# Level tables of a gated attention layer: from tables expanded by an engine to tables written run by run by transfers

## The chip, the cores and the metric

The kernel runs on one core of a Trainium2 chip. The metric is the device time of one execution in microseconds, the median of several runs. The engines of the core are TensorE (PE; PEld is its weight load), VectorE (DVE), ScalarE (ACT), GpSimd (POOL) and SyncE (SP), which here only issues transfers.

## What is computed

```python
# x: 8 batches x 1024 tokens x 128; H = 8 heads, LV = 12 levels
x = x + attn(layernorm(x)); x = x + experts(layernorm(x))
# attn, for each batch and head:
g = -softplus(x @ Wg.T + bg); G = cumsum(g, axis=1)
lam = softplus(x @ Wdl.T + Lparam)            # [b, t, h, 12]
decay = exp(G[t] - G[s]) where s <= t else 0
lamw[t, s] = lam[t, lvl(t - s)]               # lvl(0)=0, lvl(d)=floor(log2 d)+1
A = (q @ k.T / sqrt(128)) * decay * lamw
out = layernorm(concat_h(A @ v) @ Wo.T + x) * ln_g + ln_b
# experts: softmax gate, top 2 of 8 experts, weighted sum of y = x @ We[e].T + be[e]
```

## The kernel before

There are NH = 64 heads (8 batches of 8 heads), about 23 us each, and everything is fp32 in two fp32r parts, high and low. A head is a pass over NG = 12 groups (a block of 128 keys by up to 512 queries). Every group has four places, so a head has 48 places (0 to 47) and a batch 384; tables written out by hand or by a planner (`PE_MORE`, `DVE_MORE`, `ACT_MORE`, `POOL_MORE`, `Q_AT`, `V_AT`, `V_HIGH`, `V_LOW`) say at which place of the batch each engine does each extra piece. Every engine runs its list strictly in order.

For a group PE makes the scores (place 0 of the group, three matmuls into `s_ps`), DVE multiplies them with the weights `w_all` (`weigh`, `a_all`), ACT rounds the product to fp32r (`a_hi`), POOL subtracts to get the rest (`low_a`, `a_lo`, line 596), and LAG = 4 groups later PE multiplies with the values (`values`, line 1320, into `o_ps`; it waits for `a_lo`).

The weights `w_all` are exp(level logarithm + decay) and are made one head ahead, in five units (`unit(n + 1, u)` in head n, at places 2, 14, 22, 30 and 42). A unit is a chain of small f16 matmuls into `l_ps` (line 1251). Their moving operand is a table: `ra` for levels 0 to 7 and `rb` for levels 8 to 10; their stationary operand is a constant 0/1 mask. In the table each row stands for (part, level, offset q), and the row is zero except at the tokens whose offset within a run of TA = 8 (or TB = 16) tokens is q. A head has 16 matmuls of 64 columns and 16 of 56 that read `ra`, and 8 of 112, 8 of 96, 8 of 64, 2 of 320 and 2 of 192 that read `rb`: 5,120 columns. ACT then takes the exponential (`exps`, line 714), and a unit waits for the one before it to be taken.

The tables are made so: the level logarithms are stored to HBM (`ea_scratch`, `eb_scratch`) in an order in which the tokens of one offset are contiguous; SP loads them compactly (`load_e_part`, four transfers a head, lines 411 and 414) into `ea` and `eb`; POOL multiplies them, broadcast over q, with a 0/1 constant (`expand_a` at place 10, line 581, and `expand_b` at place 21, line 587). In `ra` and `rb` q is the innermost index, so a matmul reads runs of 8 or 16 contiguous f16 elements.

SP's queue in each head n, in order: at head 0 of a batch `store_out` of an earlier batch and `load_residual` (into `yx`, used by POOL's `shifted_x`, piece `xb`); at head 5 `load_x`; then `load_m(n + 3)`; at head 4 `store_el`; then `load_e(n + 4)`; in odd heads `load_n`. POOL also does most of the work of the two normalisations (`dev1`, `t_dev`, `apply1`, `t_apply`, `scale`, `xb`, `add`, `dev2`, `apply2`, `total`).

## Time and profile before

| | |
|---|---|
| median of 3 runs | 1608.88 us (1608.41 to 1609.42) |
| the profiled execution, its own time | 1608.22 us |
| its span, first to last instruction | 1606.1 us |
| granted TensorE clock, mean | 0.968 of full speed |
| PE, ACT, POOL, DVE busy | 91%, 71%, 71%, 64% |
| HBM traffic | 26 GB/s over the span |

A busy share is the time in which an engine has at least one instruction in work. The rows further down show single lines, engines and stretches: how long an instruction takes, and how long an engine sat idle before it and what ended the idle time.

### The profile page before, as it was taken

Reading aid. Unit: us, or ns where it says so; the run is one execution under the profiler, and the core shown is the slowest. Engines: PE = TensorE matmul, PEld = TensorE weight load, DVE = VectorE, ACT = ScalarE, POOL = GpSimd, SP = SyncE. Lnnn points to the kernel's source line nnn. Section 1 sums busy time; section 2 is a strip of 40 time slices with the busy share of each in tenths; the row PEclk is TensorE's granted clock in tenths of the full one; section 3 lists DMA queues with packets and bytes.
Section 4 is the critical chain, followed back from the end, with each engine's and each line's share of the span. In section 5 each row is a group of like instructions: output and inputs, shape, how many; then the busy total and the mean of one; then the engine's idle time right before and its main releaser. Section 6 shows DMA issues by size and latency. Waiting matters only on the chain.

```text
span 1606.1 us, 29807 instructions
## 1 busy us (share of the span) xinstructions
PE 1456.4 (91%) x10678; PEld 1210.6 (75%) x10678; DVE 1030.0 (64%) x2466; ACT 1141.3 (71%) x3299; POOL 1143.1 (71%) x1067
## 2 busy tenths in 40 slices
PE   5799997899989999899989999899998999989975
PEld 5588886778867887777877788678786887878853
DVE  5457565676657766586655866467674676647665
ACT  2689886786768767686766967678676886867631
POOL 1486779766896678956798667975679666896570
PEclk8799999999999999999999999999999999999987
DMA  5200100010100101001010010001010000100000
GB/s 176 64 18 16 39 28 15 10 37 20 36 15 7 38 22 36 13 15 42 10 35 13 25 36 20 23 16 35 23 36 12 10 26 19 36 16 28 8 8 13
DMA packets 80332, 44.01 MB, mean 27 GB/s; under 512 B 21832, under 2 KB 78522, under 8 KB 80058
## 3 DMA queue, kind: packets, MB, share of 16 engines
q1 hardware_dynamic: 79484, 41.83, 9.2%
q8 instruction: 85, 1.39, 0.4%
q14 instruction: 61, 0.50, 0.1%
q10 hardware_dynamic: 702, 0.29, 0.1%
HBM read 32.39 MB, written 9.18 MB: 26 GB/s over the span
## 4 chain that ended last, share of the span: by engine, by line
PE 55%; POOL 18%; DVE 12%; ACT 9%; issue 4%; DMA 1%; ACTq 0%; SPq 0%; POOLq 0%; DVEq 0%
PE o_ps L1320 15%; PE l_ps L1251 7%; PE s_ps L1235 6%; POOL a_lo L596 6%; PE s_ps L1237 6%; PE s_ps L1236 6%; PE aux L1235 4%; ACT w_all L714 4%; PE aux L1236 4%; PE aux L1237 4%; DVE a_all L912 2%; ACT a_hi L737 2%; POOL ra L581 2%; POOL e_rs L602 1%; POOL yx L441 1%
## 5 line engine op out<-in xcount | busy, mean ns | idle before, releaser
L596 POOL TENSOR_TENSOR a_lo<-a_all,a_hi 128x512 fp32r<-128x512 f32 (+2 forms) x640 | 709.1, 1125 | 323.9 <-ACT a_hi L737 322.7
L912 DVE TENSOR_TENSOR a_all<-s_ps,w_all 128x512 f32<-128x512 f32 (+3 forms) x768 | 422.6, 554 | 488.4 <-PE s_ps L1237 476.3
L714 ACT ACTIVATE w_all<-l_ps,bias 128x128 f32<-128x128 f32 x2304 | 628.5, 386 | 58.1 <-PE l_ps L1251 57.5
L737 ACT ACTIVATE a_hi<-a_all 128x512 fp32r<-128x512 f32 (+2 forms) x640 | 364.0, 591 | 254.8 <-DVE a_all L912 251.5
L1320 PE MATMUL o_ps<-a_hi,v_all 128*128 128x512 f32 (+2 forms) x1280 | 472.1, 373 | 56.9 <-POOL a_lo L596 56.8
L1320 PEld LDWEIGHTS o_ps<-a_hi,v_all 128*128 128x128 f32 x1280 | 243.9, 191 | 110.5 <-POOL a_lo L596 72.5
L1235 PE MATMUL s_ps<-q_hi,xt_hi 128*128 128x512 f32 (+3 forms) x768 | 290.4, 378 | 2.5 <-DVE a_all L912 2.5
L1236 PE MATMUL s_ps<-q_lo,xt_hi 128*128 128x512 f32 (+3 forms) x768 | 268.3, 349 | 0.0
L1237 PE MATMUL s_ps<-q_hi,xt_lo 128*128 128x512 f32 (+3 forms) x768 | 268.0, 349 | 0.0
L1320 PE MATMUL o_ps<-a_lo,v_all 128*128 128x512 f32 (+2 forms) x640 | 232.4, 363 | 0.0
L1237 PEld LDWEIGHTS s_ps<-q_hi,xt_lo 128*128 128x128 f32 x768 | 147.0, 191 | 17.1
L1235 PEld LDWEIGHTS s_ps<-q_hi,xt_hi 128*128 128x128 f32 x768 | 147.6, 192 | 15.9 <-DVE a_all L912 4.0
L1251 PE MATMUL l_ps<-rb,mask 96*128 96x112 f16 (+4 forms) x1792 | 134.7, 216 | 25.3 <-ACT w_all L714 25.3
L1236 PEld LDWEIGHTS s_ps<-q_lo,xt_hi 128*128 128x128 f32 x768 | 148.2, 193 | 11.3
L1251 PEld LDWEIGHTS l_ps<-rb,mask 96*128 96x128 f16 x1792 | 94.8, 98 | 68.0 <-ACT w_all L714 36.8
L581 POOL TENSOR_TENSOR ra<-ea,cst 128x1024 f16<-128x1024 f16 x64 | 123.3, 1926 | 29.5 <-DMA eb<-eb_scratch 29.5
L1320 PEld LDWEIGHTS o_ps<-a_lo,v_all 128*128 128x128 f32 x640 | 122.5, 191 | 12.0
L587 POOL TENSOR_TENSOR rb<-eb,cst 96x1024 f16<-96x1024 f16 x64 | 123.0, 1923 | 0.0
L899 DVE TENSOR_TENSOR v_all<-aux,v_all 128x512 fp32r<-128x512 f32 x128 | 87.3, 682 | 24.2 <-ACT v_all L729 24.2
L891 DVE TENSOR_TENSOR q_lo<-aux,q_hi 128x512 fp32r<-128x512 f32 x128 | 88.5, 691 | 4.4
L1251 PEld LDWEIGHTS l_ps<-ra,mask 128*128 128x128 f16 x2048 | 75.1, 98 | 18.2 <-issue 2.9
L889 DVE CAST q_hi<-aux 128x512 fp32r<-128x512 f32 x128 | 87.7, 685 | 0.4 <-PE aux L1237 0.3
(175 smaller groups left out, 2216.1 us busy)
## 6 DMA issues: line engine op xcount, KB each, us to landing
mt<-m_scratch SPq DMA_DIRECT2D x62, 128.0 KB, 2.0
nt<-n_scratch SPq DMA_DIRECT2D x62, 128.0 KB, 2.6
tx<-in_L_attn_x SPq DMA_DIRECT2D x9, 512.0 KB, 4.1
out<-yn SPq DMA_DIRECT2D x16, 256.0 KB, 2.3
yx<-in_L_attn_x SPq DMA_DIRECT2D x7, 512.0 KB, 4.2
ea<-ea_scratch SPq DMA_DIRECT2D x126, 16.0 KB, 1.9
eb<-eb_scratch SPq DMA_DIRECT2D x126, 6.0 KB, 1.8
ea_scratch<-tx SPq DMA_DIRECT2D x15, 128.0 KB
```

The costliest lines, as they stand in the source:

```text
L581: pool.tensor_tensor(ra[k][:, :, :, :].rearrange("p i n q -> p (i n) q"), ea[k][:, :, None].broadcast_to([P, P, TA]), c("dma")[:, None, :] ...
L587: pool.tensor_tensor(rb[k][:, :, :, :].rearrange("p i n q -> p (i n) q"), eb[k][:, :, None].broadcast_to([KB, NC * NTB, TB]), c("dmb", KB) ...
L596: pool.tensor_tensor(a_lo[r][:, 0:t1 - t0], a[r][:, 0:t1 - t0], a_hi[r][:, 0:t1 - t0].bitcast(F32), ALU.subtract).then_inc(a_lo_done, 1)
L714: last = act.activation(w[k][:, W_AT[j] + dd, :].rearrange("p (f c) -> p f c", f=2), l_ps[:, :, slot * HF:(slot + 1) * HF], ACT.Exp, bias= ...
L737: act.activation(a_hi[r][:, 0:t1 - t0], a[r][:, 0:t1 - t0], ACT.Copy).then_inc(a_hi_done, 1)
L891: dve.tensor_tensor(q_lo[n % 2][:, cols], bank(piece), q_hi[n % 2][:, cols].bitcast(F32), ALU.subtract).then_inc(freed(piece), 1)
L912: dve.tensor_tensor(a[(n * NG + g) % NA][:, 0:t1 - t0], s_ps[:, g % 2, 0:t1 - t0], w[n % 2][:, at:at + (t1 - t0) // P, :].rearrange("p i n ...
L1235: pe.matmul(o, a_hi, hi, start=True, stop=False)
L1236: pe.matmul(o, a_hi, lo, start=False, stop=False)
L1237: return pe.matmul(o, a_lo, hi, start=False, stop=True)
L1251: r = pe.matmul(o, lhsT, rhs, start=not started[f], stop=True, skip_group_check=True)
L1320: last = pe.matmul(o, lhs[:, vr, j, :], rhs[r][:, 0:t1 - t0], start=False, stop=True, skip_group_check=True)
```

## The change

The compact tiles `ea` and `eb`, the two expansions on POOL and their constants are gone. `ra` and `rb` are set to zero once at the start by four memsets on POOL. After that, every head's transfers write only the run of each offset q: 8 transfers of 16 rows of 256 bytes for `ra` (`load_ra`), and 16 transfers of 6 rows of 128 bytes for `rb` (`load_rb`), 24 in place of 4. In the tables q is now the outermost index of a row, so that a run is contiguous; the matmuls read them through a rearranged view, with q innermost, where neighbouring columns are 256 bytes (`ra`) or 128 bytes (`rb`) apart. The order of the rows (level, part, offset) and of the scratch tensors changes to fit. A head's transfers (`load_levels(n + 3)`) now wait for `l_mm`, the last unit of the head that used the buffer before, which runs at place 42; before, `load_e(n + 4)` waited for `expand_b` at place 21. At the start the transfers are shared out between SP and ACT. The planner's tables differ: two `t_apply` and one `apply2` pieces (two tiles each) of each batch go from POOL to ACT, and many pieces of all engines move by a few places.

```diff
-    l_a, q_a = (row // TA % LOW)[:, None, None], (row % TA)[:, None, None]
+    l_a, q_a = (row // 2 % LOW)[:, None, None], (row // (2 * LOW))[:, None, None]
...
     rb = np.arange(KB)
-    l_b, q_b = (rb // TB % HIGH + LOW)[:, None, None], (rb % TB)[:, None, None]
+    l_b, q_b = (rb // 2 % HIGH + LOW)[:, None, None], (rb // (2 * HIGH))[:, None, None]
...
-    put("dma", (row % TA)[:, None] == np.arange(TA)[None, :])
-    put("dmb", (rb % TB)[:, None] == np.arange(TB)[None, :])
...
-    ea_dram = nc.dram_tensor("ea_scratch", [B, 2, H * LOW, T], F16, kind="Internal").ap()
-    eb_dram = nc.dram_tensor("eb_scratch", [B, 2, H * HIGH, T], F16, kind="Internal").ap()
+    ea_dram = nc.dram_tensor("ea_scratch", [B, H * LOW, 2, T], F16, kind="Internal").ap()
+    eb_dram = nc.dram_tensor("eb_scratch", [B, H * HIGH, 2, T], F16, kind="Internal").ap()
     with ExitStack() as outer:
...
-Q_AT = {6: 0, 20: 1}
-V_AT = {11: 0, 26: 1, 36: 2, 46: 3}
-V_HIGH = {9: 0, 28: 1, 37: 2, 45: 3}
-V_LOW = {18: 0, 32: 1, 41: 2, 49: 3}
-EXPAND_A, EXPAND_B = 10, 21
+Q_AT = {5: 0, 20: 1}
+V_AT = {11: 0, 26: 1, 40: 2, 46: 3}
+V_HIGH = {9: 0, 27: 1, 40: 2, 45: 3}
+V_LOW = {19: 0, 32: 1, 41: 2, 50: 3}
...
-ACT_MORE = {13: [('y', 0)], 24: [('y', 1)], 92: [('t_high', 0)], 120: [('t_high', 1)], 124: [('x_high', 0)],
-            128: [('x_high', 1)], 136: [('abs', 0)], 140: [('num', 0)], 156: [('exp', 0)], 162: [('ln', 0)],
-            186: [('lnl', 0)], 204: [('l_high', 0)], 220: [('l_high', 1)]}
...
+ACT_MORE = {8: [('y', 0)], 28: [('y', 1)], 52: [('t_apply', 2)], 70: [('t_apply', 1)], 96: [('t_high', 0)],
+            104: [('apply2', 3)], 121: [('x_high', 0)], 124: [('t_high', 1)], 132: [('x_high', 1)],
+            141: [('abs', 0)], 145: [('num', 0)], 161: [('exp', 0)], 165: [('ln', 0)], 186: [('lnl', 0)],
+            196: [('l_high', 0)], 209: [('l_high', 1)]}
...
-POOL_MORE = {32: [('dev1', 0)], 37: [('xb', 0)], 41: [('t_dev', 0)], 44: [('xb', 1)],
-             48: [('apply1', 0), ('apply1', 1)], 49: [('scale', 0)], 52: [('apply1', 2), ('apply1', 3)],
-             56: [('add', 0)], 60: [('scale', 1)], 61: [('add', 1)], 69: [('t_apply', 0)], 73: [('t_apply', 1)],
-             77: [('t_apply', 2)], 81: [('t_apply', 3)], 93: [('dev2', 0)], 96: [('apply2', 0)], 97: [('apply2', 1)],
...
+POOL_MORE = {29: [('xb', 0)], 32: [('dev1', 0)], 33: [('apply1', 1)], 36: [('xb', 1)], 40: [('t_dev', 0)],
+             48: [('apply1', 0)], 49: [('apply1', 2), ('scale', 0)], 56: [('add', 0)], 57: [('apply1', 3)],
+             60: [('scale', 1)], 64: [('t_apply', 0)], 73: [('add', 1)], 81: [('t_apply', 3)], 93: [('dev2', 0)],
+             100: [('apply2', 2)], 101: [('apply2', 0)], 105: [('apply2', 1)], 284: [('total', 0)],
+             369: [('total', 1)]}
...
-        ea = [sb(f"ea{k}", [P, P], F16) for k in range(2)]
-        eb = [sb(f"eb{k}", [KB, NC * NTB], F16) for k in range(2)]
-        ra = [sb(f"ra{k}", [P, NC, NTA, TA], F16) for k in range(2)]
-        rb = [sb(f"rb{k}", [KB, NC, NTB, TB], F16) for k in range(2)]
+        ra = [sb(f"ra{k}", [P, TA, NC, NTA], F16) for k in range(2)]
+        rb = [sb(f"rb{k}", [KB, TB, NC, NTB], F16) for k in range(2)]
...
-        E_IN, EL = 4 * 16, 4 * 16
+        RA_IN, RB_IN, EL = TA * 16, TB * 16, 4 * 16
...
         def store_el_part(eng, b, part):
             src = (elt_hi, elt_lo)[part]
-            eng.dma_start(ea_dram[b, part], src[0:NA_ROWS, :]).then_inc(t["stored"], 16)
-            eng.dma_start(eb_dram[b, part], src[NA_ROWS:NE_ROWS, :]).then_inc(t["stored"], 16)
-
-        def load_e_part(eng, n, part):
+            eng.dma_start(ea_dram[b, :, part], src[0:NA_ROWS, :]).then_inc(t["stored"], 16)
+            eng.dma_start(eb_dram[b, :, part], src[NA_ROWS:NE_ROWS, :]).then_inc(t["stored"], 16)
+
+        def load_ra(eng, n, qs):
             b, h = divmod(n, H)
-            k = n % 2
-            eng.dma_start(ea[k][part * LOW * TA:(part + 1) * LOW * TA, :],
-                          ea_dram[b, part, h * LOW:(h + 1) * LOW, :]
-                          .rearrange("l (q n) -> (l q) n", q=TA)).then_inc(e_in[k], 16)
-            eng.dma_start(eb[k][part * HIGH * TB:(part + 1) * HIGH * TB, :],
-                          eb_dram[b, part, h * HIGH:(h + 1) * HIGH, :]
-                          .rearrange("l (q n) -> (l q) n", q=TB)).then_inc(e_in[k], 16)
+            for q in qs:
+                eng.dma_start(ra[n % 2][q * 2 * LOW:(q + 1) * 2 * LOW, q].rearrange("r i t -> r (i t)"),
+                              ea_dram[b, h * LOW:(h + 1) * LOW, :, q * T // TA:(q + 1) * T // TA]
+                              .rearrange("l r t -> (l r) t")).then_inc(ra_in[n % 2], 16)
+
+        def load_rb(eng, n, qs):
+            b, h = divmod(n, H)
+            for q in qs:
+                eng.dma_start(rb[n % 2][q * 2 * HIGH:(q + 1) * 2 * HIGH, q].rearrange("r i t -> r (i t)"),
+                              eb_dram[b, h * HIGH:(h + 1) * HIGH, :, q * T // TB:(q + 1) * T // TB]
+                              .rearrange("l r t -> (l r) t")).then_inc(rb_in[n % 2], 16)
         EL_ROWS = ((0, NA_ROWS, TA), (NA_ROWS, NE_ROWS, TB))
...
                     for part in range(2):
                     for part in range(2):
                         store_el_part(sp, b, part)
-                def load_e(n):
+                def load_levels(n):
                     if n >= 2:
-                        sp.wait_ge(rb_ready, n - 1)
+                        sp.wait_ge(l_mm, NU * (n - 1))
                     sp.wait_ge(t["stored"], EL * (n // H + 1))
-                    for part in range(2):
-                        load_e_part(sp, n, part)
+                    load_ra(sp, n, range(TA))
+                    load_rb(sp, n, range(TB))
                 def load_last_x():
...
                 sp.wait_ge(t["el_lo"], 2)
                 store_el_part(sp, 0, 1)
                 sp.wait_ge(t["stored"], EL)
-                for n in range(2):
-                    load_e_part(sp, n, 1)
+                sp.wait_ge(zeroed, 4)
+                load_ra(sp, 0, range(TA))
+                load_rb(sp, 0, range(HALF_B, TB))
+                load_ra(sp, 1, range(TA))
                 sp.wait_ge(s_hi, 2)
                 sp.wait_ge(s_lo, 2)
                 first_n()
                 store_weights(1)
                 sp.wait_ge(s_mst, 16)
+                load_rb(sp, 1, range(TB))
                 load_m(2)
-                for n in range(2, 4):
-                    load_e(n)
                 sp.wait_ge(s_nst, 64)
                 load_n(1)
                 load_x(1)
+                load_levels(2)
                 for n in range(NH):
                     b, h = divmod(n, H)
                     if h == 0:
...
                         load_m(n + 3)
                     if h == 4 and b + 1 < B:
                         store_el(b + 1)
-                    if n + 4 < NH:
-                        load_e(n + 4)
+                    if n + 3 < NH:
+                        load_levels(n + 3)
                     if n % 2 and n + 3 < NH:
                         load_n((n + 1) // 2 + 1)
...
             @block.gpsimd
             def _(pool):
-                def expand_a(n):
-                    k = n % 2
-                    pool.wait_ge(e_in[k], E_IN * (n // 2 + 1))
-                    if n >= 2:
-                        pool.wait_ge(l_mm, NU * (n - 1))
-                    pool.tensor_tensor(ra[k][:, :, :, :].rearrange("p i n q -> p (i n) q"),
-                                       ea[k][:, :, None].broadcast_to([P, P, TA]),
-                                       c("dma")[:, None, :].broadcast_to([P, P, TA]), ALU.mult).then_inc(ra_ready, 1)
-
-                def expand_b(n):
-                    k = n % 2
-                    pool.tensor_tensor(rb[k][:, :, :, :].rearrange("p i n q -> p (i n) q"),
-                                       eb[k][:, :, None].broadcast_to([KB, NC * NTB, TB]),
-                                       c("dmb", KB)[:, None, :].broadcast_to([KB, NC * NTB, TB]),
-                                       ALU.mult).then_inc(rb_ready, 1)
-
                 def low_a(n, g):
                     j, t0, t1 = GROUPS[g]
...
                 pool.memset(minus, -1.0).then_inc(s_ones, 1)
                 pool.memset(mhalf[:, :], -0.5).then_inc(ready, 1)
+                for k in range(2):
+                    pool.memset(ra[k][:, :, :, :], 0.0).then_inc(zeroed, 1)
+                    pool.memset(rb[k][:, :, :, :], 0.0).then_inc(zeroed, 1)
                 pool.wait_ge(ready, 2)
                 token_deviation(0)
                 for i0 in range(HC, NC, 2):
                     token_apply(pool, 0, i0)
-                for n in range(2):
-                    expand_a(n)
-                    expand_b(n)
                 for n in range(NH):
                     b, h = divmod(n, H)
                     for place in range(4 * NG):
                         if place % 4 == 1 and place // 4 in SPLIT:
                             low_a(n, place // 4)
-                        if place == EXPAND_A and n + 2 < NH:
-                            expand_a(n + 2)
-                        if place == EXPAND_B and n + 2 < NH:
-                            expand_b(n + 2)
                         more(b, 4 * NG * h + place)
                 for f in range(2):
                     shifted_x(B - 1, f)
...
                 act.wait_ge(t["el_hi"], 4)
                 store_el_part(act, 0, 0)
                 act.wait_ge(t["stored"], EL)
-                for n in range(2):
-                    load_e_part(act, n, 0)
+                act.wait_ge(zeroed, 4)
+                load_rb(act, 0, range(HALF_B))
                 act.activation(mhalf_exp[:, :], mhalf[:, :], ACT.Exp).then_inc(s_exp, 1)
                 act.wait_ge(s_n, 1)
                 act.activation(mn[:, :, 2, :], per_head(pn[:, :]), ACT.Copy).then_inc(s_hi, 1)
...
                 def unit(n, u):
                     k = n % 2
                     if u == 0:
-                        pe.wait_ge(ra_ready, n + 1)
+                        pe.wait_ge(ra_in[k], RA_IN * (n // 2 + 1))
                     if u == 1:
-                        pe.wait_ge(rb_ready, n + 1)
+                        pe.wait_ge(rb_in[k], RB_IN * (n // 2 + 1))
                     if n or u:
                         pe.wait_ge(w_done, n * NU + u)
                     started = [False, False]
...
                             for tb in range(NTA):
                                 f, at = divmod(tb * TA, HF)
                                 last = mm(f, l_bank[f][:, :, at:at + TA], m(f"ma{d}")[:, tb * P:(tb + 1) * P],
-                                          ra[k][:, i0:i0 + cnt, tb, :])
+                                          ra[k][:, :, i0:i0 + cnt, tb].rearrange("p q i -> p i q"))
                         if d in (1, 2, 4):
                             for tb in range(NTB):
                                 f, at = divmod(tb * TB, HF)
                                 last = mm(f, l_bank[f][:, :, at:at + TB], m(f"mb{d}", KB)[:, tb * P:(tb + 1) * P],
-                                          rb[k][:, i0:i0 + cnt, tb, :])
+                                          rb[k][:, :, i0:i0 + cnt, tb].rearrange("p q i -> p i q"))
                         if d in (3, 5):
                             for f in range(2):
-                                last = mm(f, l_bank[f], m("m9" if d == 3 else "m10", KB),
-                                          rb[k][:, i0:i0 + cnt, f * NTB // 2:(f + 1) * NTB // 2, :].rearrange(
-                                              "p i n q -> p i (n q)"))
+                                last = mm(f, l_bank[f].rearrange("p i (t q) -> p i t q", q=TB),
+                                          m("m9" if d == 3 else "m10", KB),
+                                          rb[k][:, :, i0:i0 + cnt, f * NTB // 2:(f + 1) * NTB // 2].rearrange(
+                                              "p q i t -> p i t q"))
                         slot += cnt
                     last.then_inc(l_mm, 1)
```

## Rows read from the trace of the kernel before

**Rows 1.** The page: span, and busy time of the engines (share of the span).

```profile
span 1606.1 us, 29807 instructions
...
PE 1456.4 (91%) x10678; PEld 1210.6 (75%) x10678; DVE 1030.0 (64%) x2466; ACT 1141.3 (71%) x3299; POOL 1143.1 (71%) x1067
```

**Rows 2.** Busy time in stretches: the steady one, then two neighbouring heads.

```profile
core 0: us, PE busy (x) PEld busy (x) DVE busy (x) ACT busy (x) POOL busy (x), PEclk, DMA share, GB/s
64.00:1563.00 1499.00, 1395.22 (x10412) 1164.48 (x10411) 974.37 (x2292) 1110.51 (x3230) 1124.97 (x1041) 0.98 0.08 23
...
801.25:821.04 19.79, 19.19 (x150) 15.96 (x149) 15.02 (x49) 15.71 (x49) 15.75 (x13) 1.00 0.22 63
821.04:848.00 26.96, 20.78 (x152) 17.02 (x151) 11.81 (x26) 16.93 (x51) 26.82 (x32) 0.94 0.03 7
```

**Rows 3.** Waits of PE, 64 to 1563 us (us in total, times, longest).

```profile
PE o_ps L1320 <- POOL a_lo L596: 56.8, 62, 2.1
PE l_ps L1251 <- ACT w_all L714: 20.8, 25, 2.3
PE aux L1364 <- POOL tx L441: 6.7, 6, 1.2
```

**Rows 4.** Groups of instructions by line: the expansions.

```profile
L581 POOL TENSOR_TENSOR ra<-ea,cst 128x1024 f16<-128x1024 f16 x64 | 123.3, 1926 | 29.5 <-DMA eb<-eb_scratch 29.5
L587 POOL TENSOR_TENSOR rb<-eb,cst 96x1024 f16<-96x1024 f16 x64 | 123.0, 1923 | 0.0
```

**Rows 5.** Timeline of PE, the second unit of a steady head (start, length).

```profile
806.40 0.58 PE L1251 MATMUL l_ps<-ra,mask 128*128 128x56 f16 x16
806.81 0.56 PE L1251 MATMUL l_ps<-rb,mask 96*128 96x112 f16 x8
807.18 0.36 PE L1235 MATMUL s_ps<-q_hi,xt_hi 128*128 128x256 f32 x1
```

**Rows 6.** Timeline of PE, the same unit at the start, clock at its lower level.

```profile
50.89 0.97 PE L1251 MATMUL l_ps<-ra,mask 128*128 128x56 f16 x16
51.68 0.93 PE L1251 MATMUL l_ps<-rb,mask 96*128 96x112 f16 x8
52.38 0.56 PE L1235 MATMUL aux<-nt,xt_hi 128*128 128x256 f32 x1
```

**Rows 7.** Groups by line: DVE reads with a stride (L997) and without (L912).

```profile
L997 DVE TENSOR_TENSOR tx<-aux,tx 64x512 f16<-64x512 f32 x16 | 10.8, 674 | 0.0
L912 DVE TENSOR_TENSOR a_all<-s_ps,w_all 128x512 f32<-128x512 f32 x384 | 264.0, 688 | 330.2 <-PE s_ps L1237 319.9 <-ACT w_all L714 9.1
L912 DVE TENSOR_TENSOR a_all<-s_ps,w_all 128x128 f32<-128x128 f32 x128 | 36.6, 286 | 42.8 <-PE s_ps L1237 42.8
```

**Rows 8.** One line's transfers: issue time on SP's queue (min/median/max ns).

```profile
L411 SPq DMA_DIRECT2D ea<-ea_scratch x126: 450/460/1541, 39.9 to 1461.2; - x126
L414 SPq DMA_DIRECT2D eb<-eb_scratch x126: 579/584/1549, 40.4 to 1461.7; - x126
```

**Rows 9.** Timeline of SP's queue: the start, and head 0 of a batch.

```profile
39.92 0.48 SPq L411 DMA_DIRECT2D ea<-ea_scratch  x1
...
46.38 1.33 SPq L482 DMA_DIRECT2D nt<-v_all  x2
...
811.47 0.40 SPq L498 DMA_DIRECT2D yx<-in_L_attn_x  x1
```

**Rows 10.** The page's transfers (KB each, us from issue to landing).

```profile
yx<-in_L_attn_x SPq DMA_DIRECT2D x7, 512.0 KB, 4.2
```

**Rows 11.** Groups by line: one normalising step on POOL and on ACT.

```profile
L441 POOL TENSOR_SCALAR yx<-yn,e_rs,e_sh 128x128 f32<-128x128 f32 x56 | 24.5, 449 | 0.7
...
L786 ACT ACTIVATE yx<-yn,e_sh,e_rs 128x128 f32<-128x128 f32 x8 | 3.3, 482 | 7.3 <-POOL e_sh L617 7.3
```

**Rows 12.** Timeline of POOL and of ACT in the first 60 us.

```profile
9.25 1.67 POOL L602 TENSOR_TENSOR t_rs<-t_ve,mhalf 128x8 f32<-128x8 f32 x1 [8.15 <-DVE t_ve L435]
...
53.41 0.60 ACT L729 ACTIVATE v_all<-aux 128x512 fp32r<-128x512 f32 x1 [4.50 <-DMA n_scratch<-v_all]
```

More of the change, by code:

```diff
@@ L69 @@
 for _name, _n in (("ma0", NTA * P), ("ma1", NTA * P), ("mb1", NTB * P), ("mb2", NTB * P), ("mb4", NTB * P),
-                  ("m9", P), ("m10", P), ("ident", P), ("tri", P), ("suf", P), ("dma", TA), ("dmb", TB),
-                  ("first", E), ("neg", P)):
+                  ("m9", P), ("m10", P), ("ident", P), ("tri", P), ("suf", P), ("first", E), ("neg", P)):
     CONST[_name] = (_at, _at + _n)
@@ L165 @@
 NE_ROWS = NLV * H
+HALF_B = TB // 2
 NGATE = 18
@@ new lines @@
+V_AT = {11: 0, 26: 1, 40: 2, 46: 3}
+Q_OUT = {12: 0, 22: 1}
+V_HIGH = {9: 0, 27: 1, 40: 2, 45: 3}
+V_LOW = {19: 0, 32: 1, 41: 2, 50: 3}
+PE_MORE = {9: [('Y', 0)], 21: [('Y', 1)], 90: [('T', 0)], 110: [('Z', 0)], 122: [('X', 0), ('T', 1)],
[4 rows of a table added]
+DVE_MORE = {5: [('t_stat', 0), ('t_stat', 1)], 13: [('t_stat', 3)], 16: [('t_stat', 2)],
+            17: [('o', 1), ('stat1', 0)], 29: [('stat1', 2), ('stat1', 3)], 32: [('stat1', 1)], 33: [('mean1', 0)],
+            44: [('t_mean', 0)], 77: [('stat2', 1), ('stat2', 0)], 88: [('stat2', 3)], 93: [('stat2', 2)],
+            100: [('mean2', 0)], 101: [('t_low', 0)], 113: [('z', 0)], 120: [('t_low', 1)], 129: [('x_low', 0)],
+            141: [('z', 1), ('x_low', 1)], 145: [('gate', 0)], 152: [('gate', 1)], 169: [('gate', 2), ('gate', 3)],
+            173: [('softplus', 0), ('softplus', 1)], 177: [('guard', 0)], 181: [('sums', 0)], 189: [('decay', 0)],
+            196: [('log', 0)], 197: [('log', 1)], 205: [('l_low', 0)], 220: [('l_low', 1)], 221: [('up', 0)],
[3 rows of a table added]
@@ L341, in main_stage @@
         s_cat, s_rows, s_fwg, s_wes, s_wetc = (sem(n) for n in ("s_cat", "s_rows", "s_fwg", "s_wes", "s_wetc"))
-        e_in, m_in = ([sem(f"{n}{k}") for k in range(2)] for n in ("e_in", "m_in"))
-        ra_ready, rb_ready, l_mm, w_done = sem("ra_ready"), sem("rb_ready"), sem("l_mm"), sem("w_done")
+        ra_in, rb_in, m_in = ([sem(f"{n}{k}") for k in range(2)] for n in ("ra_in", "rb_in", "m_in"))
+        l_mm, w_done, zeroed = sem("l_mm"), sem("w_done"), sem("zeroed")
         s_mm, a_done, a_hi_done, a_lo_done = sem("s_mm"), sem("a_done"), sem("a_hi_done"), sem("a_lo_done")
```

10 lines of the change are left out of this document (removed), and 15 rows, old and new, of tables (DVE_MORE, PE_MORE).

## The prediction

> **What bounds the kernel now.** I read the page first, for who is busy, then the busy times by stretch, then PE's waits. PE is the busiest engine, 1456.4 of 1606.1 us [rows 1]. In the steady stretch, which is nearly the whole run, it works for 1395.2 of 1499 us, so 103.8 us are idle [rows 2]. The reader is to see there how uneven this is: one head takes 19.8 us with PE busy for 19.2 and POOL for 15.8, and the next takes 27.0 us with PE busy for 20.8 and POOL for 26.8. That second head is set by POOL, the others by PE. The waits agree: of PE's idle time 56.8 us end with POOL's `a_lo`, 6.7 with POOL's normalised `tx` and 20.8 with ACT's exponentials [rows 3]. So two prices matter: what each PE column costs in 63 heads, and what POOL carries in about one head of eight.
>
> **POOL's share, removed.** The two expansions take 1.93 and 1.92 us a head, 246 us in all [rows 4]. Six tiles a batch leave POOL as well: 6 x 0.449 = 2.7 us a batch, 19 us over seven batches [rows 11]. The POOL-bound stretch of each batch loses up to two heads' expansions (7.7 us) and those 2.7 us, more than the 6.2 us that PE idles there [rows 2]. The gain can't exceed the waits on POOL, 56.8 + 6.7 = 63.5 us. A part stays, since `a_lo` also waits for ACT and DVE before it: I take 80% of the 63.5, -51 us (bounds: 0, if ACT's `a_hi` is late instead, to -64).
>
> **ACT's share, added.** The same six tiles cost 0.482 us each there [rows 11], 2.9 us a batch, 20 us in all. ACT is idle for 389 us of the steady stretch [rows 2], which covers them; without cover they delay an exponential that PE waits for. I take +5 (0 to +20) where PE isn't slower, and nothing where it is.
>
> **PE's columns, slower.** The matmuls of a head's units read 5,120 columns. Nothing is added in columns, instructions or weight loads, but the moving operand, until now runs of 8 or 16 adjacent f16 elements, becomes one element every 256 or 128 bytes. No matmul in this trace reads so; the price has to be bounded. The second unit shows today's: its 16 x 56 and 8 x 112 columns, 1,792, take from 806.40 to 807.18, 0.78 us or 0.435 ns a column; they are set by columns, since half the instructions take the same time when each has twice the columns [rows 5]. Lower bound: a stride is free, as on DVE, where a read with a stride of 32 bytes takes 674 ns and a contiguous one of 512 elements 688 [rows 7]. That DVE, however, takes an element only every (688 - 286) / 384 = 1.05 ns, and no engine here takes separate elements at PE's 0.435. Upper bound: PE gets them no faster than DVE, 1.05 ns a column: 5,120 x 0.61 = 3.1 us a head, +197 over 63 heads. Between the two lies the rate at which PE itself runs at its lower clock, where the same unit takes 50.89 to 52.38, 1.49 us or 0.83 ns a column [rows 6]. I take this one: it is the nearest row of the same instructions, and close to the pace at which DVE gets single elements. It costs 0.71 us on 1,792 columns, 2.03 us on 5,120, and +128 us over 63 heads (the first head's units run mostly at the lower clock already). PE is the bound in most heads, so nothing hides it; what it hides is the idle time of PE, since others now have 2 us more a head: with it half of the 20.8 us of waits on ACT goes, -10.
>
> The Trainium skill, "Advanced Engine Details and Errata", section "SBUF Cachelines", says that a line holds 16 bytes and that two hits on it are needed for full speed, and speaks of a penalty where each access goes to another line. Before, the runs fill whole lines; after, every column is on another one. The page gives no size. By it the sum is on the slow side; without it the sum is that of the first rival. DVE's strided read, which is from PSUM, doesn't show the penalty at DVE's own pace, so the trace neither confirms nor refutes the rule for PE.
>
> **SP's queue.** Issuing one table transfer takes 0.46 to 0.58 us [rows 8]. A head had four, 2.1 us; now 8 x 0.46 + 16 x 0.58 = 13.0 us, of a head of 20 to 27 us, so SP keeps up. They start after the unit at place 42 and end some 13 us on, about place 24 of the next head; the table is wanted a whole head later. What lies behind them is late: `load_n` (has another head's time), `store_out`, and `load_residual` in head 0 of a batch. It was issued at 811.47, 10.2 us after that head's first unit [rows 2, 9]; it now goes out about 12 us after, and lands 4.2 us later [rows 10], at 16. POOL wants it at place 29 (before, 37), which at 0.41 us a place (19.8 / 48) is 11 us after. POOL's `a_lo`s then queue behind `xb`, for up to 5 us, of which the lag of four groups (6.6 us less some 3 us of work) absorbs most: +10 for seven batches (0 to +25).
>
> **The start.** SP issued 4 transfers from 39.92 and then `first_n` at 46.38 [rows 9]. Now 16 `ra` runs and 8 `rb` runs stand ahead: 7.4 + 4.6 = 12.0 us, so `first_n` goes at 51.9, +5.5 us. ACT waited for the stores behind it until 53.41 [rows 12], so this is on the path. ACT's own 8 transfers, some 5 us from 39.9, end before. The memsets stand on POOL where it idles for 8.15 us before 9.25 [rows 12]; even at an expansion's 1.92 us each, four take 7.7. The first unit no longer waits for an expansion, but for seven more issues. I take +5.5 (0 to +8).
>
> The bytes stay the same (32 KB and 12 KB a head) at a DMA share of 0.08 [rows 2]: no cost. The other moved pieces change no work; nothing for them, +-5.
>
> **Sum.** Against the profiled execution's own 1608.2 us: +128 -51 -10 +10 +5.5 = 1690.7; its run lies 0.7 below the median of the runs shown, so I write 1690.
>
> **Rivals.** First, the stride is free for PE. Then 1608.2 -51 +5 +10 +5.5 +0.7 = 1578, faster by 1.9%. For it: PE already reads fp32r at the same pace as f16, so bandwidth in bytes isn't tight, and DVE's stride costs nothing. Against it: no row shows separate elements delivered in 0.435 ns. It turns at a price of about 0.1 ns a column: 5,120 x 63 x 0.1 = 32 us eat the gain; below that it decides for faster.
> Second, SP becomes the bound: if an issue with only 6 rows takes 1 us instead of 0.58, a head needs 8 x 0.46 + 16 + 1.5 = 21 us of queue, more than the light heads of 19.8; with buffers late in half of the heads by 1 to 2 us and a free stride, about 1578 + 50 = 1628; with the stride's price it is partly hidden. Against: the slowest median issue in the trace is 0.58.
> Third, the work leaves POOL but PE's waits turn to ACT's `a_hi` and exponentials (ACT gains work, is 74% busy in the steady stretch), with a free or nearly free stride: no gain, 1608 + 5 + 5.5 - 10, about 1608.
> Fourth, single elements come only at DVE's pace: 1690 + 69 = 1759.
>
> **How the numbers follow.** Price of the stride near half pace (between 0.7 and 0.95 ns a column): 0.52, around 1690, own range 1650 to 1720. Slower still: 0.06. Free stride with the gain: 0.32, around 1578. Waits turned or prices that cancel: 0.07, of which 0.05 within the bound of 0.2% (about what can be told from no change here). SP as the bound: 0.03. So slower 0.62, same 0.05, faster 0.33. Because both signs are likely, the range reaches from just below the free stride's 1578 to the top of the likeliest: 1560 to 1720.
>
> **What would show it.** The first look is the second unit's matmuls: 16 of 56 columns and 8 of 112 that take 1.5 us from first to the next group's scores, not 0.78, and a PE busy time up by some 130 us. If they take 0.8, the forecast is wrong and the first rival right. Right for POOL: busy near 880 us, waits on `a_lo` under 15 us, and the batch's second head no longer 27 us. SP: issues at 0.46 to 0.58, bursts of 13 us, and `xb` idle on the transfer into `yx`. The start: the first scores about 5 us later than now.

## The result, and the profile after

The changed kernel takes 1939.66 us (1930.96 to 1943.26, 4 runs) against 1608.64 us: a ratio of 1.205, interval 1.201 to 1.209. I had said 1690 us and a range of 1560 to 1720. The direction was right, the size was not: the loss is 331 us, where I forecast 81. The profiled execution is the shortest of the four (its own time 1930.96, span 1929.1).

The page of the changed kernel, against [rows 1]; below it the share of PE in the chain that ended last, the chain followed back from the last instruction (before the change PE had 55% of it and POOL 18%):

```profile
span 1929.1 us, 30902 instructions
...
PE 1865.5 (97%) x10678; PEld 1517.9 (79%) x10678; DVE 1021.2 (53%) x2466; ACT 1173.6 (61%) x3341; POOL 890.8 (46%) x901
...
PE 91%; ACT 4%; DVE 2%; DMA 1%; SPq 1%; issue 0%; ACTq 0%; POOL 0%; POOLq 0%; DVEq 0%
PE l_ps L1232 31%; PE o_ps L1302 20%; PE s_ps L1217 7%; PE s_ps L1218 7%; PE s_ps L1216 7%; PE aux L1216 5%; PE aux L1217 5%; PE aux L1218 5%; ACT w_all L695 2%; PE o_ps L1297 1%; ACT L695 0%; ACT L737 0%; PE aux L1377 0%; PE aux L1339 0%; PE aux L1390 0%; PE aux L1389 0%
```

PE has the same 10,678 matmuls and is busy 409 us longer. One line holds 31% of the chain, the level matmuls (L1232; L1251 before). The steady stretch, against [rows 2], and that line alone in it:

```profile
64.00:1880.00 1816.00, 1804.04 (x10429) 1472.46 (x10428) 961.79 (x2271) 1146.88 (x3287) 872.19 (x867) 0.97 0.07 19
...
64.00:1880.00 1816.00, 647.23 (x3917) 407.77 (x3915) 0.97 0.07 19
```

The level matmuls take 647 us here; the same view of the kernel before gives 226.09 us for 3,906 of them, so they are busy 421 us longer. PE as a whole is busy 409 us longer in the stretch and its idle time fell from 103.8 to 12.0 us: the stretch grew by 317 us, and what lies around it by 6, together the 323 us between the two spans. The 421 can't be set beside the 409 as they stand, since a busy time includes the end of each matmul, which overlaps the start of the next. Counted from each matmul's start to the next one's over the whole trace, idle time apart, the matmuls that read `ra` and `rb` take 526.5 us where they took 144.9: +382. All other matmuls take 27 us more, and PE's idle time between matmuls is 86 us less.

PE's timeline in the second unit of a steady head, against [rows 5]:

```profile
927.00 1.79 PE L1232 MATMUL l_ps<-ra,mask 128*128 128x56 f16 x16
928.61 1.73 PE L1232 MATMUL l_ps<-rb,mask 96*128 96x112 f16 x8
930.01 0.56 PE L1216 MATMUL s_ps<-q_hi,xt_hi 128*128 128x256 f32 x1
```

and of the same unit at the start, against [rows 6]:

```profile
54.22 1.83 PE L1232 MATMUL l_ps<-ra,mask 128*128 128x56 f16 x16
55.87 1.73 PE L1232 MATMUL l_ps<-rb,mask 96*128 96x112 f16 x8
57.27 0.56 PE L1216 MATMUL aux<-nt,xt_hi 128*128 128x256 f32 x1
```

The unit takes 3.01 us from first matmul to the next group, 1.68 ns a column in place of 0.435. The start shows how such a price is recognised: the fp32r matmuls around it are at the lower clock, yet the unit takes 3.05 us, the same, where the kernel before took 1.49 us there and 0.78 us at the upper level. The price of these columns doesn't follow PE's granted clock. The two ends of my bound, 0.435 and 1.05 ns, both lay below it.

A second cost follows from the first. Behind the same unit PE's fp32r matmuls are slow for 3.4 us, and the row of that stretch has the granted clock at its lower level (0.51 over these 3.5 us, 1.00 in the 16.7 us behind them):

```profile
930.80 0.63 PE L1302 MATMUL o_ps<-a_hi,v_all 128*128 128x512 f32 x1
931.23 0.63 PE L1302 MATMUL o_ps<-a_lo,v_all 128*128 128x512 f32 x1
...
934.02 0.40 PE L1302 MATMUL o_ps<-a_hi,v_all 128*128 128x512 f32 x1
934.25 0.39 PE L1302 MATMUL o_ps<-a_lo,v_all 128*128 128x512 f32 x1
```

```profile
929.80:933.30 3.50, 3.50 (x12) 2.90 (x11) 0.42 (x1) 2.22 (x8) 0.63 (x1) 0.51 0.00 0
```

The same 512 columns take 0.43 us there and 0.23 us later. Between 80 and 1870 us the clock falls 28 times, and 27 of these falls begin around the last matmul of a head's second unit, none over 1.1 us after its start. What this costs in all is worked out in the experiments.

The groups by line and shape give most of the list (the kernel before had the first two at 41.2 and 37.3 us, and the three of `rb` at 36.0, 33.0 and 26.0; the two shapes left out, 320 and 192 columns, rose from 28.9 and 21.3 to 79.2 and 53.1):

```profile
L1232 PE MATMUL l_ps<-ra,mask 128*128 128x64 f16 x1024 | 129.9, 295 | 0.0
L1232 PE MATMUL l_ps<-ra,mask 128*128 128x56 f16 x1024 | 114.4, 279 | 0.0
L1232 PE MATMUL l_ps<-rb,mask 96*128 96x112 f16 x512 | 110.7, 371 | 0.0
L1232 PE MATMUL l_ps<-rb,mask 96*128 96x96 f16 x512 | 95.0, 340 | 0.7 <-ACT w_all L695 0.7
L1232 PE MATMUL l_ps<-rb,mask 96*128 96x64 f16 x512 | 67.6, 287 | 3.8 <-ACT w_all L695 3.8
```

What PE waited for in the stretch, against [rows 3]; then the timeline of SP's queue with the first value weights at the start and one head's transfers, against [rows 9]; then the transfers' issue times by tile (min/median/max ns), against [rows 8]:

```profile
PE l_ps L1232 <- ACT w_all L695: 8.6, 18, 1.8
PE aux L1339 <- DVE yx L903: 2.9, 1, 2.9
PE o_ps L1302 <- POOL a_lo L581: 0.5, 1, 0.5
```

```profile
49.72 1.32 SPq L481 DMA_DIRECT2D nt<-v_all  x2
...
915.93 3.56 SPq L406 DMA_DIRECT2D ra<-ea_scratch  x8
919.53 5.40 SPq L413 DMA_DIRECT2D rb<-eb_scratch  x16
```

```profile
L406 SPq DMA_DIRECT2D ra<-ea_scratch x512: 302/420/1799, 39.7 to 1802.5; - x171
...
L413 SPq DMA_DIRECT2D rb<-eb_scratch x1016: 257/295/1477, 43.4 to 1808.1; - x170
```

POOL has left PE's waits altogether. SP's 24 transfers take 9.0 us a head, and no wait of PE in the steady stretch ends with them; at the start PE waits for `ra` once, 1.9 us, where it waited 2.2 us for POOL's expansion.

### The profile page after: what moved, and what is told of

It is laid out like the page before. It is cut to its first block, busy times and chain, and to the rows that moved or that the text cites. A ratio compares the mean times of both kernels' runs of the same rounds, so it can differ in the third digit from the quotient of the medians.

```text
span 1929.1 us, 30902 instructions
## 1 busy us (share of the span) xinstructions
PE 1865.5 (97%) x10678; PEld 1517.9 (79%) x10678; DVE 1021.2 (53%) x2466; ACT 1173.6 (61%) x3341; POOL 890.8 (46%) x901
## 4 chain that ended last, share of the span: by engine, by line
PE 91%; ACT 4%; DVE 2%; DMA 1%; SPq 1%; issue 0%; ACTq 0%; POOL 0%; POOLq 0%; DVEq 0%
PE l_ps L1232 31%; PE o_ps L1302 20%; PE s_ps L1217 7%; PE s_ps L1218 7%; PE s_ps L1216 7%; PE aux L1216 5%; PE aux L1217 5%; PE aux L1218 5%; ACT w_all L695 2%; PE o_ps L1297 1%; ACT L695 0%; ACT L737 0%; PE aux L1377 0%; PE aux L1339 0%; PE aux L1390 0%; PE aux L1389 0%
## 5 line engine op out<-in xcount | busy, mean ns | idle before, releaser
L1232 PE MATMUL l_ps<-rb,mask 96*128 96x112 f16 (+4 forms) x1792 | 394.3, 372 | 9.7 <-ACT w_all L695 9.7
L1216 PE MATMUL s_ps<-q_hi,xt_hi 128*128 128x512 f32 (+3 forms) x768 | 314.6, 410 | 0.0
L1232 PEld LDWEIGHTS l_ps<-rb,mask 96*128 96x128 f16 x1792 | 186.5, 111 | 148.5 <-issue 83.4
L1302 PEld LDWEIGHTS o_ps<-a_hi,v_all 128*128 128x128 f32 x1280 | 248.1, 194 | 37.3 <-POOL a_lo L581 4.6
L1217 PE MATMUL s_ps<-q_lo,xt_hi 128*128 128x512 f32 (+3 forms) x768 | 274.9, 358 | 0.0
L1218 PE MATMUL s_ps<-q_hi,xt_lo 128*128 128x512 f32 (+3 forms) x768 | 274.3, 357 | 0.0
L1232 PE MATMUL l_ps<-ra,mask 128*128 128x64 f16 (+1 forms) x2048 | 244.2, 287 | 0.0
L1232 PEld LDWEIGHTS l_ps<-ra,mask 128*128 128x128 f16 x2048 | 220.5, 115 | 16.6 <-issue 0.8
L1216 PEld LDWEIGHTS s_ps<-q_hi,xt_hi 128*128 128x128 f32 x768 | 156.4, 204 | 30.4 <-issue 10.1
L1217 PEld LDWEIGHTS s_ps<-q_lo,xt_hi 128*128 128x128 f32 x768 | 155.1, 202 | 18.6
L1074 DVE SCALAR_TENSOR_TENSOR yn<-aux,gl,yn 128x128 f32<-128x128 f32 x256 | 87.5, 342 | 0.0
```

Source lines behind the costliest of these rows:

```text
L1216: pe.matmul(o, a_hi, hi, start=True, stop=False)
L1217: pe.matmul(o, a_hi, lo, start=False, stop=False)
L1218: return pe.matmul(o, a_lo, hi, start=False, stop=True)
L1232: r = pe.matmul(o, lhsT, rhs, start=not started[f], stop=True, skip_group_check=True)
L1302: last = pe.matmul(o, lhs[:, vr, j, :], rhs[r][:, 0:t1 - t0], start=False, stop=True, skip_group_check=True)
```

## The experiments

Where a kernel reads wrong columns, the bias of the diagonal blocks is also multiplied by 0, so that no exponential overflows; instructions and shapes stay. All times stand beside runs of the kernel before on the same chip.

**Adjacent columns in the changed kernel.** `every` takes n x q columns that are `step` elements apart.

```diff
+                def every(table, step, n, q):
+                    flat = table[:, :, :, :].rearrange("p q i t -> p (q i t)")[:, 0:n * q * step]
+                    return flat.rearrange("p (i q s) -> p i q s", q=q, s=step)[:, :, :, 0]
...
-                                          ra[k][:, :, i0:i0 + cnt, tb].rearrange("p q i -> p i q"))
+                                          every(ra[k], 1, cnt, TA))
...
-                                          rb[k][:, :, i0:i0 + cnt, tb].rearrange("p q i -> p i q"))
+                                          every(rb[k], 1, cnt, TB))
```

> The changed kernel, except that every level matmul reads as many adjacent columns of its table as it read separate ones (the wrong columns of the right table; and the bias of the diagonal blocks is multiplied by 0 so that nothing overflows, so the output isn't the reference's). Transfers, zeroed tables, places and instruction counts stay. Theory A (the loss is PE's reading of single elements, and nothing else): the level matmuls fall from about 638 us of PE busy to about 230, the second unit from 3.0 us to 0.78, and the time is 1560 to 1590 us, the price of my first rival. Theory B (the 24 small transfers a head, their waits, or the new places cost a large part): it stays above 1650 us although PE's matmuls are short again.

Measured: 1548.98 us, ratio 0.962 (0.9603 to 0.9636). The level matmuls take 226.5 us in 64 to 1500 us. With its transfers, zeroed tables, waits and places, the changed kernel would be 60 us faster than the kernel before; its reads cost 391 us. Theory A holds in what it says of the cause, with a time below its range. The level matmuls by shape, as they are when reads cost nothing extra:

```profile
L1236 PE MATMUL l_ps<-ra,mask 128*128 128x64 f16 x1024 | 40.7, 194 | 0.0
L1236 PE MATMUL l_ps<-ra,mask 128*128 128x56 f16 x1024 | 37.3, 188 | 0.0
L1236 PE MATMUL l_ps<-rb,mask 96*128 96x112 f16 x512 | 36.0, 213 | 0.0
```

**The reads alone, in the kernel before.** The compact loads, the expansions on POOL and the places stay.

```diff
-                                          ra[k][:, i0:i0 + cnt, tb, :])
+                                          ra[k][:, :, :, :].rearrange("p i n q -> p (i n q)").rearrange(
+                                              "p (q i t) -> p i q t", q=TA, t=NTA)[:, i0:i0 + cnt, :, tb])
```

(and the same for `rb`)

> The kernel before, with its compact transfers, its expansions on POOL and its places, except that the level matmuls read their tables with the changed kernel's steps (256 or 128 bytes between neighbouring columns; wrong elements, and the diagonal bias multiplied by 0, so the output isn't the reference's). Theory A: 1880 to 1945 us, level matmuls about 640 us busy, the price of the reads on its own being about 5.96 us a head or 375 us, less the idle time of PE that it fills. Theory B: below 1750 us.

Measured: 1966.5 us, ratio 1.222 (1.2202 to 1.2239), somewhat above theory A's range, and 27 us above the changed kernel, whose transfers and places gain something beside the reads. Each shape costs what it does in the changed kernel:

```profile
L1251 PE MATMUL l_ps<-ra,mask 128*128 128x64 f16 x1024 | 130.0, 295 | 0.0
L1251 PE MATMUL l_ps<-ra,mask 128*128 128x56 f16 x1024 | 114.4, 279 | 0.0
L1251 PE MATMUL l_ps<-rb,mask 96*128 96x112 f16 x512 | 110.7, 371 | 0.0
```

So the price belongs to the access pattern, not to who wrote the table. The two runs together rule theory B out. They also show the second cost. PE's time in us over the whole trace, from each matmul's start to the next one's:

| | before | before, reads apart | changed, adjacent | changed |
|---|---|---|---|---|
| level matmuls (`ra`, `rb`) | 144.9 | 527.2 | 146.2 | 526.5 |
| all other matmuls | 1311.1 | 1359.1 | 1286.1 | 1338.6 |
| of these, at the lower clock | 68.9 | 167.0 | 42.2 | 145.5 |
| idle between matmuls | 138.3 | 70.4 | 103.4 | 52.1 |

The two pairs that differ only in the reads agree: the level matmuls take 380 and 382 us more, the others 52 and 48 us more, and the idle time falls by 51 and 68 us. The others have the same columns; what changed is that they spend 103 and 98 us more at the lower clock, where columns take about twice as long, and half of that is their loss. So about 50 of the 391 us are paid by matmuls that don't read these tables. Theory A's range had no such term, and that is why the measured time lies above it.

**Places alone.** The kernel before with the new tables of places.

```diff
-Q_AT = {6: 0, 20: 1}
+Q_AT = {5: 0, 20: 1}
...
-            128: [('x_high', 1)], 136: [('abs', 0)], 140: [('num', 0)], 156: [('exp', 0)], 162: [('ln', 0)],
+            104: [('apply2', 3)], 121: [('x_high', 0)], 124: [('t_high', 1)], 132: [('x_high', 1)],
```

> The kernel before with the changed kernel's tables of places alone (three normalising pieces a batch on ACT, others moved a few places), expansions on POOL kept. My prediction gave the moved pieces nothing (+-5 us) beside the 2.7 us a batch that leave POOL. Theory A: 1590 to 1615 us. Theory B (the places are part of the loss): above 1640 us.

Measured: 1578.93 us, ratio 0.9812 (0.9797 to 0.9827): 30 us faster, below theory A's range. I had priced the moved order at nothing. PE's wait for `a_lo` fell from 56.8 to 42.0 us over the whole run, and the 6.7 us for the normalised `tx` are gone from its longest waits:

```profile
PE o_ps L1320 <- POOL a_lo L596: 42.0, 43, 3.0
PE l_ps L1251 <- ACT w_all L714: 26.8, 22, 2.7
```

**Only the three normalising pieces on ACT**, at places 52, 70 and 104; nothing else of the places.

```diff
-ACT_MORE = {13: [('y', 0)], 24: [('y', 1)], 92: [('t_high', 0)],
+ACT_MORE = {13: [('y', 0)], 24: [('y', 1)], 52: [('t_apply', 2)], 70: [('t_apply', 1)], 92: [('t_high', 0)],
+            104: [('apply2', 3)],
```

> The kernel before with only the three normalising pieces of a batch moved from POOL to ACT (at the changed kernel's places 52, 70 and 104), nothing else. Theory E (the gain of the new places is this relief of POOL in the head that it bounds, at most 2.7 us a batch): 1585 to 1595 us, about 15 to 20 us off. Theory F (the gain comes from when the other pieces are done): 1603 us or more, with the rest of the 30 us in the order.

Measured: 1593.93 us, ratio 0.9906 (0.9891 to 0.992): 15 us. That is theory E's number; the other half of the 30 us is in the order, so neither theory has it alone.

**How far apart may columns be?** Three kernels with `every` at other steps, for `ra` and `rb` (the matmuls of 320 and 192 columns read adjacent ones), and one with adjacent groups of 2 or 4, each on its own 16 bytes:

```diff
+                def groups(table, g, n, q):
+                    flat = table[:, :, :, :].rearrange("p q i t -> p (q i t)")
+                    return flat[:, 0:n * q // g * 8].rearrange("p (i a s) -> p i a s", a=q // g, s=8)[:, :, :, 0:g]
...
-                                          ra[k][:, :, i0:i0 + cnt, tb].rearrange("p q i -> p i q"))
+                                          groups(ra[k], 2, cnt, TA))
...
-                                          rb[k][:, :, i0:i0 + cnt, tb].rearrange("p q i -> p i q"))
+                                          groups(rb[k], 4, cnt, TB))
```

> The kernel of the run adjacent (wrong columns, diagonal bias 0), with neighbouring columns 2 f16 elements (4 bytes) apart for ra and 4 (8 bytes) apart for rb in the units of 64 to 112 columns; the matmuls of 320 and 192 columns read adjacent ones. Theory A1 (the price is set by whether a 16-byte group of the table serves at least two neighbouring columns): no change, 40.7 and 37.3 us busy for ra, 36.0, 32.9 and 25.8 for rb, time about 1549. Theory A2 (PE fetches some bytes per column in proportion to the step, or a step of any kind ends the fast way): rb's three groups at 8 bytes rise clearly, to 1.5 times or more, and ra's too.

> As before with 4 elements (8 bytes) for ra and 8 (16 bytes) for rb. A1: ra unchanged at about 41 and 37 us, rb at the full price of the changed kernel, 110.7, 95.0 and 67.6 us. A2: ra dearer as well, rb perhaps half way.

> 8 elements (16 bytes) for ra, 2 (4 bytes) for rb. A1: ra at the changed kernel's 129.9 and 114.4 us, rb unchanged at 36.0, 32.9 and 25.8. A2: ra below that, since 16 bytes is far less than the 256 of the changed kernel.

> Neighbouring columns in adjacent groups of 2 f16 elements for ra and of 4 for rb, each group 16 bytes from the next (wrong columns, diagonal bias 0). A1: two columns for a fetch, so both tables stay near the fast price (ra 41 and 37 us, rb 36, 33 and 26). If instead each 16-byte group costs a fixed time of some 1.6 ns whatever is taken from it, ra costs 0.8 ns a column, about 75 and 66 us, and rb 0.4, unchanged; this would also explain the 12 us that tiles_inner lies above adjacent, whose groups of 3 to 7 elements come close to that limit.

One execution each: 1588.8, 1728.0, 1679.6 and 1591.1 us, so no time here has an interval. The verdict rests on the second unit in PE's timeline, at the upper level of the clock in all four. `ra` 4 bytes and `rb` 8 bytes apart, then 8 and 16, then 16 and 4, then groups of 2 and of 4:

```profile
713.97 0.58 PE L1236 MATMUL l_ps<-ra,mask 128*128 128x56 f16 x16
714.39 0.98 PE L1236 MATMUL l_ps<-rb,mask 96*128 96x112 f16 x8
715.13 0.37 PE L1216 MATMUL s_ps<-q_hi,xt_hi 128*128 128x256 f32 x1
```

```profile
721.53 1.01 PE L1236 MATMUL l_ps<-ra,mask 128*128 128x56 f16 x16
722.36 1.78 PE L1236 MATMUL l_ps<-rb,mask 96*128 96x112 f16 x8
723.81 0.38 PE L1216 MATMUL aux<-wcat_hi,xt_hi 128*128 128x104 f32 x1
```

```profile
730.41 1.79 PE L1236 MATMUL l_ps<-ra,mask 128*128 128x56 f16 x16
732.02 0.58 PE L1236 MATMUL l_ps<-rb,mask 96*128 96x112 f16 x8
732.42 0.36 PE L1216 MATMUL s_ps<-q_hi,xt_hi 128*128 128x256 f32 x1
```

```profile
713.91 1.01 PE L1236 MATMUL l_ps<-ra,mask 128*128 128x56 f16 x16
714.74 0.58 PE L1236 MATMUL l_ps<-rb,mask 96*128 96x112 f16 x8
715.13 0.36 PE L1216 MATMUL s_ps<-q_hi,xt_hi 128*128 128x256 f32 x1
```

Each of the two parts has 896 columns, so a difference of starts divided by 896 is the time of a column:

| columns side by side in 16 bytes | `ra`, ns a column | `rb`, ns a column |
|---|---|---|
| 4 (step 4 bytes; `rb` also groups of 4) | 0.47 | 0.45, 0.44 |
| 2 (step 8 bytes; `ra` also groups of 2) | 0.93, 0.93 | 0.83 |
| 1 (step 16 bytes) | 1.80 | 1.62 |
| 1 (256 or 128 bytes, the changed kernel) | 1.80 | 1.56 |

Theory A1 fails at its number, two: two columns for each 16 bytes still cost double. A2 fails as well, since 16 bytes cost as much as 256, and a step of 4 bytes nothing. What fits all of it is the alternative in the last expectation: every 16 bytes that a matmul reads cost about 1.6 to 1.8 ns, whatever is taken from them, and a column at least 0.43 ns; from four columns on, the second is the bound. In these runs only one of the two tables is at the full price, and the mean granted clock stays at 0.973 to 0.978, as with adjacent columns; the frequent falls were seen only with both at the full price. Why, the runs don't tell.

**Tiles innermost.** That suggests a version which keeps the direct transfers and reads side by side. The tile index goes last in the scratch order, in the tables and in the PSUM bank; ACT does the stepping.

```diff
-        ra = [sb(f"ra{k}", [P, TA, NC, NTA], F16) for k in range(2)]
+        ra = [sb(f"ra{k}", [P, TA, NTA, NC], F16) for k in range(2)]
...
-            n = T // q // 2
-            return src[r0:r1, :].rearrange("r (q n) -> r q n", q=q)[:, :, f * n:(f + 1) * n]
+            return src[r0:r1, :].rearrange("r (q t i) -> r q t i", q=q, i=NC)[:, :, :, f * HC:(f + 1) * HC]
...
-                                    l_ps[:, :, slot * HF:(slot + 1) * HF], ACT.Exp,
+                                    l_ps[:, :, at * HF:(at + cnt) * HF].rearrange(
+                                        "p f (c i) -> p f c i", i=cnt)[:, :, :, i - i0], ACT.Exp,
...
-                                          ra[k][:, :, i0:i0 + cnt, tb].rearrange("p q i -> p i q"))
+                                          ra[k][:, :, tb, i0:i0 + cnt])
```

> The changed kernel with the tile index innermost, in the scratch order, in the tables and in the PSUM bank of a unit: a run of one offset is still one contiguous transfer, a matmul reads 3 to 8 adjacent f16 elements of one 16-byte group at a time and writes PSUM contiguously, and ACT reads PSUM with a step of 12 to 32 bytes; it computes the reference. Theory A, with the price set by how many neighbouring columns lie side by side: 1560 to 1590 us, level matmuls 230 to 260 us busy. If groups of 3 to 5 elements are too short, the units with 3, 4 and 5 tiles stay slow and the time is 1600 to 1700. Theory B: above 1650. If ACT's stepped read costs, the exponentials' 385 ns goes up by 50 ns or more.

Measured: 1561.77 us, ratio 0.9702 (0.9688 to 0.9717), faster than both kernels. The level matmuls by shape (the 64 columns of `rb` left out), and the exponentials whose read of PSUM is now stepped:

```profile
L1233 PE MATMUL l_ps<-ra,mask 128*128 128x64 f16 x1024 | 40.9, 194 | 0.0
L1233 PE MATMUL l_ps<-ra,mask 128*128 128x56 f16 x1024 | 40.6, 194 | 0.0
L1233 PE MATMUL l_ps<-rb,mask 96*128 96x112 f16 x512 | 39.5, 220 | 0.0
L1233 PE MATMUL l_ps<-rb,mask 96*128 96x96 f16 x512 | 33.2, 208 | 1.6 <-ACT w_all L695 1.6
L1233 PE MATMUL l_ps<-rb,mask 96*128 96x320 f16 x128 | 32.9, 340 | 19.0 <-ACT w_all L695 18.9
L1233 PE MATMUL l_ps<-rb,mask 96*128 96x192 f16 x128 | 25.4, 279 | 0.0
L695 ACT ACTIVATE w_all<-l_ps,bias 128x128 f32<-128x128 f32 x2304 | 631.2, 388 | 54.6 <-PE l_ps L1233 53.8
```

ACT pays nothing (388 ns; 386 in the kernel before). PE pays a little where a group has 7, 5 or 3 columns: 40.6 us for 56 columns against 37.3 with adjacent columns, 39.5 against 36.0 for 112, 32.9 against 28.9 for 320, 25.4 against 21.4 for 192. Groups of 8, 6 and 4 pay nothing (40.9 against 40.7 for 64, 33.2 against 32.9 for 96). From start to start that is 12 us in all, nearly the whole 13 us by which this version lies above the run with adjacent columns. The size is that of one column more in each odd group: two matmuls of the same shape in a row start 29 ns apart for 56 columns as for 64; 175 ns for 320 in fives, and 6/5 of the adjacent 147 is 177; 112 ns for 192 in threes, and 4/3 of 83 is 110. The price of 16 bytes can't explain the 5 and the 7. Each odd group here also starts at an odd column, so the runs don't separate the count from the start.

**The same with the old places.** `V_LOW` and the other tables as in the kernel before.

```diff
-V_LOW = {19: 0, 32: 1, 41: 2, 50: 3}
+V_LOW = {18: 0, 32: 1, 41: 2, 49: 3}
```

> The kernel of the run tiles_inner (reference output) with the tables of places of the kernel before: the transfers' part alone, without its new places and with the price of the reads gone. The places alone took 30 us off the kernel before. Theory C (the two parts free the same resource, POOL, so that their gains overlap): 1562 to 1578 us, less than 30 us worse than tiles_inner. Theory D (they add up): 1588 to 1595 us.

Measured: 1582.7 us, ratio 0.9845 (0.9825 to 0.9864). It lies between the two theories: transfers alone give 26 us, places alone 30, both together 48, so some 8 us are the same. The 26 and the 48 still contain the 12 us of the odd groups.

**The order of the start.** `load_ra` of the second head behind the value weights.

```diff
                 load_rb(sp, 0, range(HALF_B, TB))
-                load_ra(sp, 1, range(TA))
                 sp.wait_ge(s_hi, 2)
...
                 sp.wait_ge(s_mst, 16)
+                load_ra(sp, 1, range(TA))
                 load_rb(sp, 1, range(TB))
```

> The kernel of the run tiles_inner with the eight transfers of the second head's ra table issued after the first value weights and their stores in SP's queue, not before. If SP's queue sets the start, as my prediction's term of +5.5 us says (the first load of nt went out 3.3 us later than before the change), the time falls by 3 to 4 us against tiles_inner, to about 1558; if something else sets the start, no change.

Measured: 1556.83 us, ratio 0.9678 (0.9663 to 0.9692), against 0.9702 of tiles innermost: some 4 us, as expected, though the two intervals overlap slightly. `nt` goes out where it did before the change:

```profile
46.39 1.32 SPq L480 DMA_DIRECT2D nt<-v_all  x2
```

This is the fastest version that computes the reference, 3.2% below the kernel before.

## Why the prediction was right in direction and wrong in size

**PE's columns, slower** is the step that failed: +128 us, measured +382 us in the level matmuls themselves and 391 us of the whole (changed kernel against adjacent columns). The mechanism was right: single elements cost PE time, and the idle time that hides some of it was named, though it hid 51 us and not 10. The size was off by a factor of three, for a stated reason: "PE gets them no faster than DVE, 1.05 ns a column" was used as an upper bound, but it is another engine's pace and bounds nothing for PE, whose columns came every 1.68 ns. Choosing the row of the lower clock made it worse: it gave the feel of a measured price for a read that no row showed, and the same unit now takes the same time at both levels of the clock. What stood in for the unknown was a range of 0.435 to 1.05 ns; my stated range then ended even below that (1720, with the fourth rival at 1759).

A term was missing: the slow reads bring the clock down for the fp32r matmuls behind them, about 50 us. The prediction used the lower clock only as a yardstick for a price and put its return in the steady stretch at nothing.

The rule of the Trainium skill ("Advanced Engine Details and Errata", section "SBUF Cachelines") pointed the right way and named the right 16 bytes. Its figure of two hits for full speed isn't what these runs show for PE: two hits cost 0.83 to 0.93 ns a column, four are needed for 0.44 to 0.47.

**What it hides**: I let half of PE's waits on ACT go, and they fell by 59%, from 20.8 to 8.6 us. Of those on POOL I let 80% go; with `tx` they fell from 63.5 to 0.5. With adjacent columns 24.1 us of them are left, so the relief of POOL took 39 us and the longer heads hid the rest.

**POOL's share**: -51 us for the whole relief. Transfers alone gave -26 us, or about -38 without the 12 us of the odd groups, the three pieces alone -15, and both with the new order and adjacent columns -60. The size was near, in part by luck: the relief took 39 us of waits and not 51, and "the other moved pieces change no work; nothing for them" left out about 15 us of gain. POOL was busy for 891 us, as forecast (880).

**ACT's share**, +5 where PE isn't slower: not seen by itself. Moving the three pieces made the kernel faster by 15 us, with ACT's share in it, and PE's waits on ACT in the steady stretch stayed at 20.3 us (20.8 before).

**SP's queue**: 13.0 us forecast for a head, 9.0 measured, because the smaller transfers are issued in 0.42 and 0.295 us, not in the 0.46 and 0.58 of the larger ones. "xb idle on the transfer into yx" didn't happen, in the changed kernel or in that with adjacent columns: no idle time of POOL stands before that line. The term was 0, not +10. The second rival, SP as the bound, is out.

**The start**: +5.5 forecast. `first_n` went out 3.3 us later, not 5.5, and moving one load gives about 4 us back (0.24% between two ratios).

**The first rival** said 1578 for a free stride; the kernel with adjacent columns took 1549. It would have been 29 us too slow: the +5 of ACT and the +10 of SP's queue didn't come, and the order of the places gave some 15 us that no term had. (The 0.7 us between the profiled execution and the median is added there and left out in the main sum, which would read 1691.)

## What to carry to other kernels

When a layout change makes a transfer contiguous, look at what it makes of the matmul's moving operand: count how many neighbouring columns lie in the same 16 bytes, and keep four or more f16 columns together, in even numbers and from an even column on. If an order has to be turned somewhere, let it be ACT's read of PSUM, which cost nothing here, rather than PE's read of SBUF. And a pace measured on one engine is no upper bound for another: where no row shows an access pattern, the upper end stays open, and the range must say so.

## What the runs showed of the hardware

- A moving operand of single f16 elements costs 1.56 to 1.80 ns a column, nearly the same at 16, 128 and 256 bytes between columns. At 128 and 256 bytes it is the same at both levels of PE's granted clock (3.01 and 3.05 us for the second unit).
- Two neighbouring f16 columns in each 16 bytes cost 0.83 to 0.93 ns a column, four 0.44 to 0.47. Groups of 3, 5 and 7 columns from an odd column on cost as much as groups of 4, 6 and 8.
- Issue times on SP's queue: 0.295 us for 6 rows of 128 bytes, 0.42 us for 16 rows of 256 bytes, 0.46 us for 64 rows of 256 bytes and 0.58 us for 48 rows of 128 bytes. Neither the number of rows nor the bytes alone orders them.
- An f16 memset of 128 x 1024 on POOL takes 0.95 us, as the query of one tile's instructions shows:

```profile
L658 POOL MEMSET ra<- x2: 947/949/951, 1.0 to 2.8; 128x1024 f16 x2
```

- The mean granted clock fell from 0.968 to 0.951; with the reads in the kernel before it was 0.945, with adjacent columns 0.975. In the changed kernel nearly all falls come behind the second unit, whose two tables are both read apart. Against the reads of adjacent columns the other matmuls lose 52 us, and 48 us where the kernel before reads apart.
